# State-space convolution and mixture of experts: the four channels' kernel products on four column positions, stored by four DMAs

## The reference

```python
# _L0_cond_ref: x is (B=32, H=64, L=1024), 64 channels with a state of N=64
u_m = u * mask[:, None, :]
...
K = 2.0 * jnp.einsum('hn,hnl->hl', Cs, jnp.exp(P)).real      # one kernel of 1024 steps per channel
...
y = jnp.fft.irfft(u_f * k_f, n=n)[..., :Lq]                  # causal convolution of u_m with K
y = y + u_m * D[:, None]                                     # skip weight of the channel
return y * mask[:, None, :]

# _L0_ffn_ref: 2048 rows of 1024, 16 experts, the best 2 of each row
logits = x @ gate_w.T
...
out = jnp.einsum('bei,hei,be->bh', h, d_r, w)

x = x + _L0_ffn_ref(_L0_cond_ref(x, ...), ...)
```

## Time and profile before

| | |
|---|---|
| Median of three executions | 488.37 us (484.63 to 492.79) |
| Profiled execution | 489.8 us, span 488.0 us |
| TensorE busy | 435.9 us, 89% |
| VectorE busy | 195.4 us, 40% |
| ScalarE busy | 107.9 us, 22% |
| GpSimd busy | 168.8 us, 35% |
| Moved by DMA | 115.99 MB, mean 238 GB/s |
| Granted TensorE clock, mean | 0.978 |

### The profile page before, as it was taken

One profiled execution on the slowest core, in us unless ns is written; L12 is line 12 of the kernel. 1 busy time (PEld: TensorE's weight loads), 2 busy tenths in 40 slices (PEclk: granted clock), 3 DMA queues, 4 the chain that ended last, 5 costly groups with the idle time before them and its releaser, 6 DMA issues.

```text
span 488.0 us, 9071 instructions
## 1 busy us (share of the span) xinstructions
PE 435.9 (89%) x2822; PEld 375.5 (77%) x2822; DVE 195.4 (40%) x525; ACT 107.9 (22%) x257; POOL 168.8 (35%) x213
## 2 busy tenths in 40 slices
PE   0379999999999998987899999999799999999991
PEld 0369999998989998965777888887578788887770
DVE  6932444443344434488333333332322233333330
ACT  3980010000000000071022222221222232222220
POOL 4643223322222110001772443344244663453322
PEclk9987999999999999998999999999999999999996
DMA  8977978989989998896799988978898996777650
GB/s 275 339 229 224 273 256 239 283 274 276 280 283 294 304 311 265 277 336 242 253 326 260 238 241 252 306 159 220 247 249 208 218 275 147 163 161 121 108 80 14
DMA packets 46491, 115.99 MB, mean 238 GB/s; under 512 B 10098, under 2 KB 25714, under 8 KB 46322
## 3 DMA queue, kind: packets, MB, share of 16 engines
q1 hardware_dynamic: 25138, 73.49, 47.1%
q0 software_dynamic: 12096, 33.58, 30.8%
q10 hardware_dynamic: 9216, 8.39, 5.4%
HBM read 93.63 MB, written 40.66 MB: 275 GB/s over the span
## 4 chain that ended last, share of the span: by engine, by line
PE 47%; DMA 32%; DVE 7%; issue 5%; SPq 3%; POOLq 2%; POOL 1%; ACT 1%; DVEq 0%; ACTq 0%
PE conv_ps L1058 20%; DMA out<-arena,from_row 19%; PE conv_ps L1207 12%; DMA k_rows<-k_sb 9%; PE conv_ps L1226 7%; DMA arena<-k_rows 3%; PE turn_ps L1216 3%; PE conv_ps L1165 2%; POOLq L473 2%; SPq L336 1%; POOL out L479 1%; DVE tmp L667 1%; PE turn_ps L1069 1%; SPq L335 1%; ACT arena L580 1%
## 5 line engine op out<-in xcount | busy, mean ns | idle before, releaser
L1058 PE MATMUL conv_ps<-arena 128*128 128x256 f32 (+7 forms) x1024 | 159.8, 314 | 7.6 <-DMA arena<-k_rows 7.6
L1058 PEld LDWEIGHTS conv_ps<-arena 128*128 128x128 f32 x1024 | 151.5, 196 | 15.8 <-issue 7.0
L1207 PE MATMUL conv_ps<-arena,ys_t 128*128 x640 | 127.8, 353 | 1.9 <-DVE ys_t L1005 1.9
L1207 PEld LDWEIGHTS conv_ps<-arena,ys_t 128*128 128x128 f32 x640 | 118.1, 191 | 13.5 <-issue 13.5
L479 POOL DMA_INDIRECT out<-arena,from_row x40 | 62.8, 1571 | 125.4 <-DMA out<-arena,from_row 77.1
L1226 PE MATMUL conv_ps<-arena,hid_t 112*128 x160 | 76.0, 597 | 5.2 <-DVE hid_t L1020 5.2
L772 DVE TENSOR_TENSOR arena<-conv_ps,mask_t 128x256 f32<-128x256 f32 x64 | 27.1, 424 | 91.9 <-PE conv_ps L1058 91.0
L1025 DVE TENSOR_SCALAR arena<-conv_ps,slot_weight 128x512 f32<-128x512 f32 x40 | 30.0, 751 | 70.4 <-DMA out<-arena,from_row 40.0
L1226 PEld LDWEIGHTS conv_ps<-arena,hid_t 112*128 112x128 f32 x160 | 27.3, 190 | 26.2 <-issue 26.1
L627 ACT ACTIVATE arena<-conv_ps,slot_weight 128x512 f32<-128x512 f32 x40 | 27.5, 687 | 76.2 <-DMA out<-arena,from_row 42.1
L1013 DVE TENSOR_TENSOR hid<-silu,conv_ps 128x112 f32<-128x112 f32 x40 | 10.8, 271 | 82.0 <-ACT silu L621 82.0
(11 more groups left out here) (177 smaller groups left out, 343.2 us busy)
## 6 DMA issues: line engine op xcount, KB each, us to landing
arena<-k_rows SPq DMA_DIRECT2D x64, 512.0 KB, 6.4
arena<-gu_t SPq DMA_DIRECT2D x16, 896.0 KB, 9.1
y_rows<-y_blk ACTq DMA_DIRECT2D x64, 128.0 KB, 4.5
arena<-x_time SPq DMA_DIRECT2D x56, 128.0 KB, 5.3
arena<-d_t SPq DMA_DIRECT2D x16, 448.0 KB, 11.2
arena<-x_time SPq DMA_DIRECT2D x2, 512.0 KB, 5.9
out<-arena,from_row POOLq DMA_INDIRECT x44, 7.0
out<-ys SPq DMA_DIRECT2D x1, 512.0 KB, 7.4
```

The costliest lines, as they stand in the source:

```text
L1058: last = nc.tensor.matmul(conv_ps[:, h, d * B:C * B], toep[:, p, h, d * P:(d + 1) * P], u_t[:, p, h, 0:(C - d) * B], start=(d == 0), stop= ...
L1207: last = nc.tensor.matmul(gu_ps, ys_t[:, t % 2, c, :], flat[:, bass.ds(bufs[t] * WE + c * GU, GU)], start=(c == 0), stop=(c == C - 1))
```

## The change

The products of channel h go to PSUM partitions 32 h to 32 h + 31, all in the same 32 columns, so that each channel's matmul uses a column position of its own. The copy on VectorE then has 128 partitions of 32 values in place of 32 of 128. The skip weights come as a tile of 128 partitions by 16 groups, with the weight of channel h in row 32 h and zeros elsewhere, and one column of it is added to the first column of the group's values. The store becomes four DMAs, one a channel, each of 32 partitions by 32 values; SyncE waits for all four. The number of bytes and of 128-byte pieces stored stays as it is.

```diff
-        skip_row = sb("skip_row", [1, H])
+        skip_col = sb("skip_col", [P, G])
...
-        k_sb = sb("k_sb", [LO, 2, HG, LO])
+        k_sb = sb("k_sb", [P, 2, LO])
...
-        k_ps = k_bank[0:LO, 0:HG * LO].rearrange("p (h n) -> p h n", h=HG)
+        k_ps = k_bank[:, 0:LO]
...
-            sp.dma_start(skip_row[:, :], skip).then_inc(par_in, 16)
+            sp.dma_start(skip_col[:, :], skip).then_inc(par_in, 16)
...
                 sp.wait_ge(k_added, g + 1)
-                sp.dma_start(bass.AP(k_rows, g * HG * KROW + P - 1, [[LO, LO], [KROW, HG], [1, LO]]),
-                             k_sb[:, p, :, :]).then_inc(k_stored[p], 16)
-
-                sp.wait_ge(k_stored[p], 16 * (i + 1))
+                for h in range(HG):
+                    sp.dma_start(bass.AP(k_rows, (g * HG + h) * KROW + P - 1, [[LO, LO], [1, LO]]),
+                                  k_sb[h * LO:(h + 1) * LO, p, :]).then_inc(k_stored[p], 16)
+
+                sp.wait_ge(k_stored[p], 64 * (i + 1))
                 for h in range(HG):
...
-                    dve.wait_ge(k_stored[p], 16 * i)
-                nc.vector.tensor_copy(k_sb[:, p, :, :], k_ps[:, :, :]).then_inc(k_copied, 1)
+                    dve.wait_ge(k_stored[p], 64 * i)
+                nc.vector.tensor_copy(k_sb[:, p, :], k_ps).then_inc(k_copied, 1)
                 dve.wait_ge(k_copied, g + 1)
-                nc.vector.tensor_tensor(k_sb[0:1, p, :, 0], k_sb[0:1, p, :, 0], skip_row[0:1, hs(g)],
+                nc.vector.tensor_tensor(k_sb[:, p, 0:1], k_sb[:, p, 0:1], skip_col[:, bass.ds(g, 1)],
                                         ALU.add).then_inc(k_added, 1)
...
-                    last = nc.tensor.matmul(k_ps[:, h, :], am[:, p, h, :], bm[:, p, h, :], start=True, stop=True)
+                    last = nc.tensor.matmul(k_ps[h * LO:(h + 1) * LO, :], am[:, p, h, :], bm[:, p, h, :],
+                                            start=True, stop=True)
...
-        "skip": np.asarray(L0_cond_D).reshape(1, H),
+        "skip": np.pad(np.asarray(L0_cond_D).reshape(G, HG, 1), ((0, 0), (0, 0), (0, LO - 1))).reshape(G, P).T,
```

## The result

| | before | changed |
|---|---|---|
| Median of four executions | 486.5 us (484.24 to 492.79) | 495.48 us (494.33 to 501.57) |
| Ratio | | 1.020, 95% interval 1.0144 to 1.0256 |
| Profiled execution, span | 489.8, 488.0 us | 496.39, 494.5 us |

The change makes the kernel slower by 2.0%. Six later executions beside eleven of the kernel before gave 496.11 against 487.08 us, ratio 1.0184 (1.0137 to 1.0232). The forecast had the sign, and the time is inside its range (484 to 499), but it expected +2.1 us and +9 came.

A forecast was written before the change was run, and what follows sets the result against it. Two loops of nearly the same length, TensorE's to about 98 us and then SyncE's, were taken to bound the kernel. 489.8 + 0.9 (tails) + 0.7 + 1.0 (start) - 0.5 (products) = 491.9 us profiled, median 490.5, range 484 to 499.

The forecast's parts named there:

- What bounds the kernel: Convolution stage: TensorE paces it from 33.31 to about 98 us, then mostly SyncE's queue of stores and loads to 206 us.
- Issues hidden behind the backlog: SyncE's stores, groups 1 to 15: three more issues, 1.44 us a group, cost nothing while queued loads cover them.
- The first rival: SyncE's queue: store issues are not hidden, its loop grows 1.44 us a group, time 506 us; chance 0.12.
- The tail, "I take 0.1": Stores landing behind the last load: 0.1 us more a wait, bounds 0 to 0.6; +0.9 us over 9 waits after 98 us.
- completions in turn: Rival: each extra store adds 0.2 us to every group's tail, +5.4; with start terms +8.5, 497 us; chance 0.06.
- its sign of 0.8: A tail of more than 0.8 us behind the last Toeplitz load would speak for completions landing in turn.
- Of the ones before, TensorE's pace covers it.: Store waits before 98 us (group 1 and 5 more): longer tails there cost nothing, as TensorE sets the pace.
- the start terms: Delays before the first convolution: skip weights' load +1.0 us (0 to 1.65) and group 0's stores +0.7 (0 to 1.4).
- Skip weights, +1.0: Skip load at the start, now 128 rows of 64 B: delays VectorE's first arithmetic by 1.0 us (0 to 1.65).
- Group 0's stores, +0.7: First group's store on SyncE: 1.44 us of extra issues half hidden by the x copies, +0.7 us (0 to +1.4).
- Products, -0.5: TensorE's eight passes a group: 0.08 us saved in each of groups 2 to 7, -0.5 us (0 to -1.6).

## Why the prediction was right and where not

- **What bounds the kernel.** Right in kind: two loops of nearly equal length, SyncE's on the chain from 98 us. The store ahead of the loads shows it.
- **Issues hidden behind the backlog.** Right. Four issues take 2.3 us in place of 0.6, and neither the waits by channel nor the unwaited stores cost anything clear of noise. The first rival (506 us) fell with it: from the first store to the next load's issue it is 7.8 us over groups 3 to 15, against 7.1 before and 8.4 as it asked for.
- **The tail, "I take 0.1".** This step failed. It had 0 to 0.6 us as its bounds and measured 0.57 (0.90 less 0.33), near the upper end. I argued from equal bytes and pieces; the row for it, four small stores in one queue behind a backlog, wasn't in the trace. The rival "completions in turn", 0.2 us for each further store and given 0.06, has the mechanism that came true: the run with a semaphore for each store shows them land 0.19 us apart, and the tail of 0.90 us is past its sign of 0.8.
- **"Of the ones before, TensorE's pace covers it."** This failed too. The queue had a lead of some us up to 98 us in the kernel before, and I counted it as cover in every group. It is a stock: each longer tail draws on it. In the changed kernel the lead is gone by group 4, TensorE waits 2.8 us before 98 us, and all 15 tails count, not 9: 8.5 us in place of 0.9.
- **The time.** That it lies inside the range (484 to 499) is luck more than forecast. The sum said 491.9 us for the profiled execution and 490.5 for the median, measured were 496.39 and 495.48; the range was wide by the tail's upper bound, the start terms and the scatter. The rival's 497 is close by luck as well: it is made of 5.4 us of tails and 3.1 of start, where 8.5 of tails and 0.6 of start came.
- **Skip weights, +1.0.** Its load lands 2.04 us after issue in place of 1.85: +0.19. The row of the same shape, 3.5 us for the lengths, had other loads ahead of it, so it was a bound and no estimate. I should have stayed near the lower end.
- **Group 0's stores, +0.7.** From the first store to the loads it is 6.11 us (23.69 to 29.80) against 5.76 (23.44 to 29.20): +0.35. The first convolution came 0.7 us later; I had +1.7 for both.
- **Products, -0.5.** Each group's went from 0.37 to 0.20 us, double the saving of 0.08 that I took; but from group 4 on TensorE spent it waiting for loads. The copy on VectorE took 0.18 us where I wrote 0.16.

The rows of TensorE's products in the chain, the first at a granted clock of 0.50, the second at 1.00, and of the copy:

```profile
38.65 0.27 PE k_bank L1051 x8
47.80 0.20 PE k_bank L1051 x8
...
L760 DVE COPY k_sb<-k_bank x16: 174/184/192, 23.2 to 185.3; 128x32 f32<-128x32 f32 x16
```

The estimate made by the Trainium skill, TensorEngine Tiling (Array Packing), section "Instruction Overhead", was 0.2 us for eight passes; the trace agrees with 0.20.

The sum as it came, in SyncE's queue: +0.6 at the first loads, +8.5 in the tails of groups 1 to 15, -0.4 between the loads' first issue and last landing. Behind the last convolution matmul it is -2.2 in this execution, about as much as the two traced executions of the changed kernel differ by.

## What to carry to other kernels

A small store that is waited for and stands last in a queue is paid by the landing of its last part. Splitting it cost 2% here, though its bytes stayed the same and its issues were hidden. Count such tails in every round of the loop: the lead that the queue had was used up in four rounds here, and then every tail counted. Before one trims such a wait, ask whether the small store can be issued before the large loads: here moving it gave 2%, and the change that had lost 2% then lost nothing. Four stores ahead of all loads, though, cost 6 us more than one, and with a load first they didn't, so a load should go first.

## What the runs showed of the hardware

Small stores that had been queued behind 2.5 MB of loads for 5 to 6 us didn't land together when the loads were done: with a semaphore for each they landed 0.18, 0.37, 0.56 and 0.75 us behind the last load (medians). To a waiter for all of them, three further stores of 32 pieces of 128 bytes added 0.57 us to the tail (0.55 in the old layout), three of a single piece 0.1 us in all.

The Trainium skill, DMA: Bandwidth & Descriptors, section "Anatomy of one DMA", calls the write of the semaphore at a DMA's end on this chip essentially free. No run here times that write alone. The runs say that three more DMAs with the same bytes between them are not free to one who waits for them (ratio 1.0181), and that no cost can be measured for one who doesn't wait for the last (1.0013 with waits by channel; 1.0006 with three more stores that add bytes). The prediction took the same section's fixed cost of about 2.0 us for SyncE's stores; the section gives it for DMAs issued by GpSimd. Three more of SyncE's stores cost 0.57 us a group here, not 6.
